# Twelve activation loads from GpSimd's DMA queue to ScalarE's, and four slices from GpSimd's to SyncE's: one layer of attention and ternary feed-forward on 8 cores

## What is computed

```python
xn = (x - mean) / sqrt(var + 1e-5)              # over the last axis
# attention: 16 heads of 128
q, k = rope(xn @ wq), rope(xn @ wk); v = xn @ wv
attn = softmax(causal(q @ k.T / sqrt(128)))
a = (attn @ v) @ wo
# feed-forward with ternary weights
scale = mean(abs(weight))
w_t = clip(round(weight / scale), -1, 1) * scale
y = x + a + xn @ w_t.T + bias
```

## Time and profile before

| | |
|---|---|
| median of 2 runs | 1845.43 us (1842.59 to 1848.27) |
| profiled execution | 1863.85 us |
| its span, slowest core (core 1) | 1862.3 us |
| spans of the cores 0 to 7 | 1826.9, 1862.3, 1815.1, 1829.8, 1826.9, 1836.6, 1820.5, 1835.8 |
| busy on core 1 | PE 1527.7 us (82%), DVE 761.4 (41%), ACT 476.9 (26%), POOL 102.9 (6%) |
| moved by core 1's DMA | 194.93 MB, 105 GB/s |
| loads of x in phase 1 | 16 of 1 MB, median 18.5 us to landing |
| loads of wf | 32 of 1 MB, median 7.3 us |

### The profile page before, as it was taken

One profiled execution on the slowest core, in us unless ns is written; L12 is line 12 of the kernel. 1 busy time (PEld: TensorE's weight loads), 2 busy tenths in 40 slices (PEclk: granted clock), 3 DMA queues, 4 the chain that ended last, 5 costly groups with the idle time before them and its releaser, 6 DMA issues. The chain is left out here.

```text
span 1862.3 us, 29592 instructions; the slowest of 8 cores (1815.1 to 1862.3 us)
## 1 busy us (share of the span) xinstructions
PE 1527.7 (82%) x9096; PEld 878.7 (47%) x9096; DVE 761.4 (41%) x1559; ACT 476.9 (26%) x837; POOL 102.9 (6%) x121
## 2 busy tenths in 40 slices
PE   0505057899999999999999999999828999999999
PEld 0202023344444444444444344444317788888888
DVE  2434254254454464574564564653501222222222
ACT  1000012735535514514524434434310000000000
POOL 1100001010010100000000000000000000000000
PEclk9957578999999999999999999999968999999999
DMA  8992936061661585835725725610064786875772
GB/s 156 165 106 40 133 51 130 24 114 44 120 132 45 81 156 89 130 73 92 131 66 96 133 66 75 86 22 7 9 155 95 165 169 153 183 156 134 165 149 91
DMA packets 350134, 194.93 MB, mean 105 GB/s; under 512 B 240163, under 2 KB 338468, under 8 KB 343588
## 3 DMA queue, kind: packets, MB, share of 16 engines
q0 software_dynamic: 139360, 93.33, 30.6%
q1 hardware_dynamic: 157156, 62.48, 19.0%
q10 hardware_dynamic: 53472, 37.23, 6.9%
HBM read 177.28 MB, written 32.51 MB: 113 GB/s over the span
## 5 line engine op out<-in xcount | busy, mean ns | idle before, releaser
L605 ACT ACTIVATE et<-pC,bias 128x512 bf16<-128x512 f32 (+3 forms) x240 | 149.8, 624 | 638.3 <-PE pC L592 637.3
L499 PE MATMUL pA<-xnT,wslk 128*128 128x512 bf16 x480 | 120.5, 408 | 183.8 <-DMA xnT<-xnn 183.7
L642 PE MATMUL pF<-et,onms 128*128 128x512 bf16 (+3 forms) x640 | 224.3, 352 | 16.1 <-ACT et L605 11.3
L616 DVE TENSOR_TENSOR et<-et,trim 128x128 bf16<-128x128 bf16 x256 | 57.5, 225 | 272.3 <-ACT et L605 268.1
L499 PEld LDWEIGHTS pA<-xnT,wslk 128*128 128x128 bf16 x480 | 47.8, 103 | 245.3 <-issue 201.5
L965 PE MATMUL pA<-wtc,xnT 128*128 128x256 bf16 x1024 | 123.9, 275 | 23.4 <-DMA wtc<-wtT_scr 15.8
L644 PE MATMUL pG<-et,vh 128*128 128x512 bf16 (+3 forms) x384 | 137.2, 361 | 0.0
L605 ACT ACTIVATE et<-pD,bias 128x512 bf16<-128x512 f32 (+3 forms) x208 | 130.7, 628 | 2.7 <-PE pD L592 2.3
L592 PE MATMUL pC<-qTh,kTh 128*128 128x512 bf16 (+3 forms) x240 | 84.0, 350 | 56.3 <-ACT et L605 56.3
L981 PE MATMUL pA<-woc,oTh 128*128 128x256 bf16 x896 | 109.7, 275 | 23.3 <-DMA oTh<-outT_scr 23.3
L1004 DVE TENSOR_TENSOR osl<-pA,xsl 128x256 f32<-128x256 f32 x64 | 27.2, 425 | 240.1 <-PE pA L981 136.1
(11 more groups left out here) (99 smaller groups left out, 1853.7 us busy)
## 6 DMA issues: line engine op xcount, KB each, us to landing
xst<-wf POOLq DMA_DIRECT2D x32, 1024.0 KB, 7.3
xst<-x POOLq DMA_DIRECT2D x16, 1024.0 KB, 18.5
xsl<-x SPq DMA_DIRECT2D x128, 128.0 KB, 3.9
wtc<-wtT_scr ACTq DMA_DIRECT2D x16, 1024.0 KB, 13.0
woc<-wo POOLq DMA_DIRECT2D x16, 1024.0 KB, 14.1
y<-osl ACTq DMA_DIRECT2D x128, 128.0 KB, 3.3
wslq<-wq POOLq DMA_DIRECT2D x16, 512.0 KB, 7.8
wslk<-wk POOLq DMA_DIRECT2D x16, 512.0 KB, 9.6
```

The costliest lines, as they stand in the source:

```text
L499: e.matmul(pp[:, 0:CW], wsl[:, it * 128:(it + 1) * 128], bass.AP(xnT, it * S + c * CW, [[NT * S, 128], [1, CW]]), start=(it == 0), stop=False)
L605: e.activation(out=et[slot][:, col0:CW], in_=pc_[:, col0:CW], func=AF.Exp, scale=INV_SQRT_D, bias=bias3[:, :]).then_inc(sems["ac"], 1)
L616: e.tensor_tensor(out=et[slot][:, col0:col0 + 128], in0=et[slot][:, col0:col0 + 128], in1=tri[:, :], op=ALU.mult).then_inc(sems["dv"], 1)
L642: e.matmul(pF[:, col0:CW], onm[:, :], et[slot][:, col0:CW], start=(kt == 0), stop=(kt == nkt - 1))
```

## The change

1. The loads of x for tiles 4 to 15 are issued by ACT instead of POOL, on three semaphores of their own (`y0` to `y2`). Tiles 0 to 3 stay with POOL. The loads keep their buffers and their waits.
2. In phase 2 the four slices 10 to 13 of `oTh[0]` leave POOL's list for SP's, behind the ten that stand there; the fourteen use four semaphores in turn instead of two, so four can be under way. POOL's second `woc` follows its first at once.

```diff
@@ SEM_NAMES
-             "wo0", "wo1", "xs0", "xs1", "sy0", "sy1", "dv", "ac", "pe"]
+             "wo0", "wo1", "xs0", "xs1", "sy0", "sy1", "y0", "y1", "y2",
+             "dv", "ac", "pe"]
@@ def plan_ln_tile(tt):
             b = tt % 3
             b2 = tt % 2
-            xs = "x%d" % b
-            my_x = dma("gpsimd", xs,
+            if tt < 4:
+                qname, xs = "gpsimd", "x%d" % b
+            else:
+                qname, xs = "scalar", "y%d" % b
+            my_x = dma(qname, xs,
                        (lambda tt=tt, b=b: (xst[b][:, :],
                         bass.AP(x_d.tensor, tt * 128 * E, [[E, 128], [1, E]]), False)),
                        extra_waits=[xst_free[b]])
@@ phase 2
         if chunks:
             plan_ph2_weights(0)
-        if do_ph2:
-            for hh in range(10, H - 2):
-                dma("gpsimd", OTH0[2 + (hh % 2)],
...
-                    extra_waits=(ph2_finals if hh < 12 else []))
-        if chunks:
             plan_ph2_weights(1)
...
         if do_ph2:
-            for hh in range(10):
-                dma("sync", OTH0[hh % 2],
+            for hh in range(H - 2):
+                dma("sync", OTH0[hh % 4],
...
-                    extra_waits=(ph2_finals if hh < 2 else []))
+                    extra_waits=(ph2_finals if hh < 4 else []))
```

## The result

The changed kernel takes 1829.8 us (median of 11 runs), against 1848.3 us for the kernel before, run beside it on the same chip: a ratio of 0.990, 95% interval 0.989 to 0.992.

A forecast was written before the change was run, and what follows sets the result against it. PE was taken to stand low in the first 280 us, waiting for transposes of xn, and at the change of phase. From 1836.6 us, + 26 + 5 - 4 plus 1.55 gave 1865 us, range 1831 to 1890.

The forecast's parts named there:

- The serial order: x loads of tiles 4 to 15: ACT issues each only after the previous tile's Exp; about 13 us apart, DVE waiting 10.
- L: Landing time of an x load from ACT's queue beside a transpose; bounds 5.1 to 12.3 us, taken as 9.5.
- part 1: Moving the x loads of tiles 4 to 15 to ACT: three stages 148.8 us against 122.7, +26 us.
- 21.1 + 3L: Stage length in us, from a tile group's first statistics on DVE to PE's restart; forecast 49.6 us.
- A and B: Stages before PE restarts on tiles 4 to 7 and 8 to 11; 46.9 and 45.8 us before, to lose 3 and 4.
- C: Stage before PE restarts on tiles 12 to 15; 29.9 us before, forecast to lose 20 us.
- Part 2: First tile group: tile 4's load comes earlier, beside transposes and head weights, delaying PE's first restart; +5 us.
- Part 3: Change of phase: fourteen slices on SP, four in flight, POOL's second woc at once; -4 us.
- No allowance for the unlucky core: Nothing added for the 7 us between 1838.2 and the median 1845.4, put down to loads colliding with two overlapping transposes.
- Rival 1: Stages: the load lands as if alone, L = 6; 1831 us; decides below L = 6.6; chance 0.25.
- Rival 2: Stages: the queue makes no difference, L = 12.3, three stages +51.3 us; 1890 us; chance 0.17.
- Rival 3: First group: tile 4's load costs +12 us instead of +5; 1872 us; chance 0.10.

The follow-up runs named there:

- e3: Kernel before, x loads still on POOL's queue, but each from tile 4 on waits for the Exp of the tile before: 1846.1 us, ratio 0.998.
- e5: Kernel before, x loads still on POOL, but each transpose of xn issued only when the one before it has landed: 1846.1 us, ratio 0.999.
- e10: e7's timing of the x loads, but all issued from POOL's queue, tile 3's in its old place: 1796.4 us, ratio 0.972 to the kernel before.
- e7: Kernel before, x loads from tile 3 on ACT, held until earlier transposes landed so one flies beside each stage's transposes: 1795.3 us, ratio 0.969.
- e4: Kernel before, x loads of tiles 4 to 15 on ACT's queue, three running ahead nearly as on POOL; phase 2 as before: 1817.1 us, ratio 0.982.
- e8: Changed kernel, chunk 1's two weight loads in phase 2 held until all 14 slices have landed: 1819.5 us, ratio 0.983 to the kernel before.
- e2: Kernel before with only the phase 2 changes, x loads staying on POOL: 1842.5 us, ratio 0.995.

## Why the prediction was wrong

**The serial order** was right. ACT issues a load only after the Exp of the tile before, DVE waits for each of nine, transposes land one by one, and the prefetch within a group is gone. The distance of two loads is 9 us, though, not 13, and DVE waits 4 us for each, not 10.

**The step that failed: the size of L in part 1.** The formula for a stage, 21.1 + 3L, held: with the measured L of 5.3 us it gives 37.0, and core 5 shows 37.9, 37.3 and 37.1. L is the median of core 5's loads between 85 and 250 us (the other cores' are 5.0 to 5.3):

```profile
DMA to landing us min/median/max: 4.8/5.3/5.7
```

L was taken as 9.5, "a little under the middle of 7.9 and 12.3". So core 5's three stages are 112.3 us, not 148.8; against 122.7 this is -10.4, not +26. That is all of the error and more. Both bounds had been worked out; the lower, 5.1, is where it came out. The choice between them leaned on the pair of the earlier trace rows, where the load was issued 0.49 us behind the transpose, and it took only 0.6 us off the middle of 7.9 and 12.3 for going ahead of it. Here the order decides: 1.8 us ahead the load lands nearly as if alone, and the transpose behind it pays about 1 us (5.6 in stage A against 4.6). e3 shows it on POOL's own queue: 1.0 us ahead, 6.6 us instead of 12.3. The second transpose that joined that pair is no excuse for the 12.3, as e5 shows. Why a close follower is so slow is open.

The effect of part 1 is thus the sum of two large ones of opposite sign: 11.9 and 11.3 us gained in A and B where collisions had been, 9.8 lost in C where prefetch had worked (means over the cores). "A and B lose only 3 and 4 us" had the wrong sign; C's loss was half of the 20 forecast or less (7.2 on core 5).

The section "Issuing engines are not separate DMA queues" of the Trainium skill's page "DMA: Bandwidth & Descriptors" was cited for L being the same from either queue. With loads held away from transposes the runs nearly agree (e10's stages are 1.7 us longer than e7's, the medians are 1796.4 and 1795.3). With loads and transposes mixed, e4's loads land in 7.1 us and those of the kernel before in 16.7; but they also start half a microsecond earlier against the transposes, so this isn't shown to be the queue, and it doesn't contradict the page.

**Part 2, tile 4's load, +5.** Measured -0.4 on core 5 (67.80 against 68.23) and +1.2 in the mean. The kind was right: three such loads instead of one, in e4, cost 7.1 us in the mean and 5.8 on core 5. The size of 5 was chosen between nothing and 12, and the 12 was taken from a load that flew beside transpose 0; this one comes when fewer transposes are left, which may be why it hurts less; no run tested that. The term was mis-sized by 4 us in the mean and 5 on core 5.

**Part 3, the change of phase, -4.** Measured 0 in the mean (39.8 and 39.6), worse on core 5 (39.0 to 44.7) and on core 1 (41.7 to 46.1). Of the two readings the pessimistic one came true in the changed kernel, "the last slice lands when everything has", and e8 shows that the bytes were the limit there: 10.3 us go when two loads are held. But e2, with the same phase 2 and the loads of x on POOL, shows 3.3 us gained at this place, near the forecast 4. So the term isn't refuted in general; why it vanishes beside part 1 is open.

**No allowance for the unlucky core** was right in kind: all stages of all cores now lie between 35.9 and 38.3 us. But it couldn't outweigh L. By the measured terms the sum would have been 1836.6 - 10.4 + 0 + 0 + 1.55, about 1828, and 1829.8 was measured. That these lie so close is partly luck: core 5's own span fell by 15.5 us and the slowest core's by 30, and neither is the 10.4 of the sum.

**The rivals.** Rival 1, "the load gets out of the way", came true by its mechanism. That its number (1831 for L = 6) was near too is partly luck: the stages gave 5 us more than it said, phase 2 four less. Its turning point, L = 6.6, fits e3 roughly: the loads land in 6.6 us, the three stages take 129.5 us in the mean against 124.7 before (POOL's later issue is no part of the formula), and the slowest cores come out even. Rival 2 fell with L; its 12.3 us describes rather a load close behind its transpose, as in e10's pairs on odd cores. Rival 3 fell: the first group lost 1.2 us, not 12.

## What to carry to other kernels

In these runs a load that was issued 1 to 2 us ahead of a DMA transpose cost both little; one that followed close behind, or flew among two transposes, could cost each of them several times its length. So look at the order of issue to half a microsecond, not only at what overlaps. Where each piece of work is short of nothing but latency, hold the prefetch until the transposes have landed and put it beside the engine's computing; this was worth 3% here, from either queue (0.969 and 0.972). When a bound's two ends give opposite signs, take the value from the row whose order of issue is that of the new kernel, and where there is none, let the two ends share the chance instead of taking a value between them. At a change of phase, hold back first what isn't needed yet: that gained 10.3 us here where greater depth beside part 1 had gained nothing.

## What the runs showed of the hardware

- The same transposes, 8864 packets, hold the DMA engines 28 us in one arrangement and 12.4 in another. In these windows the busy share of a DMA queue is no measure of its work.
- What a 1 MB load and a 512 KB transpose of xn do to each other depends on which goes first, and by how little. Pairs of the stages, all cores; alone, a load takes mostly 4.7 to 5.2 us and a transpose 4.2 to 4.6:

| the load's issue, against the transpose's | queue, run | load lands after | transpose |
|---|---|---|---|
| 1.7 to 1.8 us ahead | ACT, after | 4.8 to 6.8 us | 5.1 to 7.0 us |
| 1.0 to 1.1 ahead | POOL, e3 | 6.3 to 7.7 | 7.2 to 8.5 |
| the same moment | ACT, e7 | 5.7 to 7.5 | 7.6 to 9.9 |
| 0.48 behind, even cores | POOL, e10 | 7.7 to 8.6 | 8.0 to 9.0 |
| 0.48 behind, odd cores | POOL, e10 | 11.1 to 12.9 | 11.5 to 13.3 |
| 0.41 to 0.44 behind | POOL, e5 | 9.1 to 16.3 | 9.4 to 17.0 |
| 1.9 behind | POOL, e5 | 6.3 to 8.3 | 4.3 to 7.3 |
| 2.3 to 2.5 behind, four pairs | POOL, e5 | 7.2 to 19.3 | 9.5 to 21.7 |

- The queue and the order change together in most of these rows, so what is the queue's own isn't shown. The reasons are open.
- Landing times beside transposes from POOL's queue depend on the core: in the kernel before, the shortest load of a core in 85 to 250 us is 7.6 to 8.0 us on cores 0, 2, 4 and 6 and 11.4 to 11.7 on 3, 5 and 7 (10.8 on core 1). From ACT's queue in the kernel after, all eight have medians of 5.0 to 5.3. The reason is open.
